# V's loads in small pieces, V's rounding on GpSimd, and first loads and scores issued ahead of a meeting

## The chip, the cores and the metric

The kernel runs on one core of one Trainium2 chip. The metric is the device time of one launch in microseconds (us). The core has five engines that run side by side, each with its own instruction stream, and that meet only at semaphores: TensorE (PE, with the weight loads shown apart as PEld), VectorE (DVE), ScalarE (ACT), GpSimd (POOL) and SyncE (SP), which here only issues DMAs. "SPq" is SyncE's queue of DMA issues.

## What is computed

64 images (3 x 96 x 96) and 64 texts of 32 tokens become one sequence each of N = 36 + 32 = 68 tokens of 192 channels. An attention of 12 heads with fake quantization follows, then a mixture of 8 experts. The part that the change touches is the attention:

```python
def fq_act(x):
    mn = jnp.minimum(x.min(), 0.0); mx = jnp.maximum(x.max(), 0.0)
    scale = jnp.maximum((mx - mn) / 255.0, EPS)
    zp = qmin - jnp.round(mn / scale)
    return (clip(round(x / scale) + zp) - zp) * scale, scale
y, _ = fq_act(x @ fq_weight(w_qkv).T + b_qkv)      # one scale for all of Q, K, V
attn, s_attn = fq_act(einsum('bhnd,bhmd->bhnm', q, k) * hd ** -0.5)   # one scale for all scores
attn = int_log_softmax(attn, s_attn)
o, _ = fq_act(einsum('bhnm,bhmd->bhnd', attn, v))
o, _ = fq_act(o @ fq_weight(w_proj).T + b_proj)
```

Each `fq_act` needs the largest and the smallest value of a whole tensor before any of it can be rounded, so the kernel comes to a halt at each of them: all engines finish, one number is formed, all go on.

## The kernel before

**Stages.** The program is one block of five streams. `barrier(eng, name)` (line 120) is a meeting of all five: each engine drains, adds one to `all_engines_done` and waits until all have. The meetings divide the program into the embedding with Q, K and V; the first pass over the scores, which forms them only to take their extremes; the second pass, which forms them again and does softmax and the sum over V; and the output projection with the experts.

**Embedding.** `STEPS` = 29 steps each handle some tiles. `UNITS_AT` says at which step which of 16 units of tokens goes through `qkv`; `scale_v` (line 1306) on VectorE multiplies its V rows into one of two buffers `vst`, and `store_v` on SyncE writes them to the DRAM tensor `v_rows`. `scale_v(e)` waits until the rows of unit e - 2 have left the buffer (`v_saved`). `load_v` brings V back with tokens in partitions, so that `yv` has 68 partitions of 64 sequences times 192 channels. `V_LOADS` (line 218) lists these loads as (step, unit that must be stored, first sequence, end). `extremes_qkv` on VectorE takes the extremes.

**First pass.** It runs in 8 chunks of 8 sequences. ScalarE's `to_halves(c)` (line 916) scales Q and K into `qt` in 8 instructions, first the columns left of a tile of 64 rows ("Q's remainder", the last 4 of 68 tokens), then the rest. VectorE's `to_whole(c)` (line 1390) rounds the remainder (`left_whole`) and the rest into the arrays QK0 and QK1 (`qk_whole`). GpSimd spreads the remainder of every chunk over 16 columns per head with `headmask` (line 758, `qk_chunk`), in two instructions, for QK0 (128 partitions) and QK1 (64). SyncE's `load_seqs` copies sequences from QK0 and QK1 to the staging tiles `st0` and `st1` (three DMAs each), waiting for `qk_whole` and `qk_chunk`; TensorE's `scores` works on two sequences at a time (`scored`), and VectorE's `extremes(c)` (line 1407) reduces them in PSUM, four instructions for each pair, 32 pairs.

After chunk 8 ScalarE converts V (`v_added`, line 940, two instructions of 6144 elements) once all chunks are done, VectorE rounds it into `VQ` (line 1432), reduces the extremes and raises `a_minmax`. GpSimd's `reduce_pair` (line 731) takes the maximum over partitions, some 60 small VectorE instructions on `sc` form the scalars of the softmax, and four constants for the output projection follow (lines 1492 to 1495). Then comes the meeting.

**Second pass.** 32 pairs of sequences. SyncE runs `load_two`, four steps later `spread_v`, which copies V from `VQ` to `stv`, and in the last step `load_rest`, two large loads for the last stage (`hf`, 3264 KB, and `w_split`, 4032 KB). VectorE works in the fixed order of the `pipeline` call at line 1570.

## Time and profile before

| what | us |
| --- | --- |
| runs | 943.77, 942.96, 940.64 |
| median | 942.96 |
| profiled execution, its time | 945.13 |
| profiled execution, its span | 943.2 |
| VectorE busy, of the span | 709.8 |
| TensorE busy | 604.6 |
| ScalarE busy | 515.3 |
| GpSimd busy | 252.1 |

The span is what the trace covers; the execution's time has 1.9 us more around it. Times in the trace count from the span's start. No engine is busy all the time, and a meeting costs what the engine that comes last is late, so the profile is to be read stretch by stretch and at the seams between stages: there the idle time ahead of a group, and the engine that ended it, tell more than sums.

### The profile page before, as it was taken

To read this page: it belongs to the slowest core of one execution; us is meant where nothing else is said; L and a number is where in the kernel's file an instruction comes from. 1 tells how busy PE (TensorE), PEld (TensorE's weight loads), DVE (VectorE), ACT (ScalarE), POOL (GpSimd) and SP (SyncE) were. 2 spreads that over 40 slices of the span, in tenths; PEclk is the share of its full clock that TensorE was granted. 3 is DMA by queue.
4 is the path that set the end of the run, shared out by engine and by line. 5 is a ranking of instruction groups with operands and counts; after the bars stand their busy time and mean duration, and the time that the engine had idled before them with its cause. 6 is when DMAs were issued, how large, how long until landed. Compare 5 with 4: busy or idle time off the path is not lost.

```text
span 943.2 us, 19819 instructions
## 1 busy us (share of the span) xinstructions
PE 604.6 (64%) x6474; PEld 451.9 (48%) x6474; DVE 709.8 (75%) x1831; ACT 515.3 (55%) x951; POOL 252.1 (27%) x245
## 2 busy tenths in 40 slices
PE   3589889898406667058888888341222349999970
PEld 2589768776204334024555555331112237777760
DVE  2535668777548999789999999987776788667783
ACT  3122268766345424048888888454554226888840
POOL 2022111120011221012222222110355750036575
PEclk9999789999755555555565555555555569999985
DMA  7974024443222221022222222451011241467753
GB/s 172 258 202 120 18 54 131 109 119 120 96 66 82 68 68 51 9 47 33 43 43 43 43 43 37 106 220 59 33 55 58 77 147 51 140 188 218 226 168 113
DMA packets 151481, 92.77 MB, mean 98 GB/s; under 512 B 88828, under 2 KB 143684, under 8 KB 151084
## 3 DMA queue, kind: packets, MB, share of 16 engines
q1 hardware_dynamic: 143560, 72.28, 29.3%
q0 software_dynamic: 7856, 19.68, 7.2%
q8 instruction: 34, 0.56, 0.3%
q14 instruction: 31, 0.25, 0.1%
HBM read 45.62 MB, written 31.85 MB: 82 GB/s over the span
## 4 chain that ended last, share of the span: by engine, by line
DVE 28%; PE 24%; issue 17%; SPq 16%; ACT 9%; DMA 3%; POOL 2%; POOLq 0%; DVEq 0%; ACTq 0%
PE ps L1844 19%; SPq L659 8%; ACT R L806 5%; ACT R L809 3%; DVE M L1413 3%; DVE M L1414 3%; SPq L637 2%; POOL R L799 2%; SPq L636 2%; SPq L638 2%; DVE R L1403 2%; DVE R L1801 1%; PE ps L2018 1%; PE ps L2114 1%; PE ps L1869 1%
## 5 line engine op out<-in xcount | busy, mean ns | idle before, releaser
L1844 PE MATMUL ps<-R 128*128 128x256 f16 (+9 forms) x2064 | 310.2, 303 | 53.0 <-DVE R L1801 16.1
L1844 PEld LDWEIGHTS ps<-R 128*128 128x128 f16 (+5 forms) x2064 | 221.6, 129 | 113.3 <-issue 59.1
L806 ACT ACTIVATE R<-ps 128x768 f16<-128x768 f16 (+7 forms) x257 | 159.8, 649 | 93.5 <-PE ps L2018 18.9
L1844 PE MATMUL ps<-M 32*128 32x68 bf16 (+4 forms) x1196 | 100.6, 242 | 117.5 <-DMA M<-R 67.2
L1844 PEld LDWEIGHTS ps<-M 32*128 32x128 bf16 (+3 forms) x1196 | 64.9, 115 | 168.9 <-issue 66.5
L809 ACT ACTIVATE R<-R,sc 128x512 f16<-128x512 f32 (+7 forms) x107 | 83.6, 838 | 105.6 <-DVE R L1403 40.1
L799 POOL DMA_INDIRECT R<-y_by_tile,M x68 | 66.7, 981 | 98.0 <-DMA y_by_tile<-R 79.4
L771 POOL TENSOR_TENSOR R<-R,M 128x884 f32<-128x884 f32 x32 | 53.2, 1664 | 145.5 <-ACT M L958 145.5
L790 POOL DMA_INDIRECT x_by_expert<-R,M x68 | 67.2, 989 | 60.3 <-DVEq L1707 40.5
L806 ACT ACTIVATE R<-R 128x512 f16<-128x512 f32 (+4 forms) x121 | 64.1, 549 | 35.3 <-DVE R L1801 34.5
L2018 PE MATMUL ps<-ident_b,R 128*68 128x128 bf16 x416 | 53.8, 298 | 25.3 <-ACT R L806 23.9
L1844 PE MATMUL ps<-M,R 128*128 128x8 f16 (+3 forms) x358 | 38.7, 242 | 30.5 <-DVE R L1603 21.9
L2018 PEld LDWEIGHTS ps<-ident_b,R 128*68 128x68 bf16 x416 | 39.6, 160 | 33.0 <-ACT R L806 29.4
L2077 PE MATMUL ps<-ident_f,R 128*128 128x128 f16 x102 | 14.0, 309 | 60.4 <-DVE R L1652 60.4
L1806 DVE TENSOR_TENSOR R<-R 128x256 f16<-128x256 f32 x58 | 24.6, 425 | 36.5 <-ACT R L806 36.5
L1844 PE MATMUL ps<-R,M 68*32 68x4 bf16 (+3 forms) x1680 | 46.7, 208 | 3.7 <-DVE R L1314 2.5
L949 ACT ACTIVATE ps<-ps,sc 128x512 f32<-128x512 f32 x64 | 37.2, 603 | 18.2 <-PE ps L1844 17.2
L1511 DVE SCALAR_TENSOR_TENSOR R<-ps,sc,M 128x544 f16<-128x544 f32 x64 | 42.5, 706 | 6.2 <-PE ps L1844 5.6
L1844 PEld LDWEIGHTS ps<-M,R 128*128 128x128 f16 (+2 forms) x358 | 25.9, 119 | 41.2 <-issue 14.8
L741 POOL COPY R<-R 96x768 f32<-96x768 f32 x24 | 20.5, 863 | 91.0 <-PE ps L1906 91.0
L1413 DVE TENSOR_REDUCE M<-ps 128x8 f32<-128x544 f32 x64 | 41.3, 645 | 4.1 <-PE ps L1844 3.9
L1844 PEld LDWEIGHTS ps<-R,M 68*32 68x32 bf16 (+1 forms) x1680 | 36.2, 111 | 11.9 <-issue 5.0
(293 smaller groups left out, 1050.2 us busy)
## 6 DMA issues: line engine op xcount, KB each, us to landing
R<-x_by_expert SPq DMA_DIRECT2D x41, 192.0 KB, 2.6
y_by_tile<-R SPq DMA_DIRECT2D x41, 192.0 KB, 2.3
R<-in_x_dram SPq DMA_DIRECT2D x12, 576.0 KB, 9.0
M<-R SPq DMA_DIRECT2D x16, 260.0 KB, 2.3
M<-R SPq DMA_DIRECT2D x32, 130.0 KB, 2.0
R<-w_split SPq DMA_DIRECT2D x1, 4032.0 KB, 23.1
R<-h_rows SPq DMA_DIRECT2D x1, 3264.0 KB, 14.3
out_dram<-R SPq DMA_DIRECT2D x17, 192.0 KB
```

The costliest lines, as they stand in the source:

```text
L659: sp.dma_start(stv[:, par, b, a].rearrange("p (j h d) -> p j h d", h=2, d=HD)[:, :, a, :], VQ[:, bass.ds(g * 2 + b, 1), :].rearrange("p o ...
L771: pool.tensor_tensor(L[par], L[par], S[:, par, 1, :].unsqueeze(2).to_broadcast([P, SLOTS, N]), ALU.subtract).then_inc(sem("relative"), 1)
L790: pool.indirect_dma_start(xg, bass.IndirectOffsetOnAxis(ap=slot[:, n, k:k + 1], axis=0), rows2[:, n, :], None).then_inc(sem("scattered"), 16)
L799: pool.indirect_dma_start(gb[:, i % 4, j, k, :], None, yg[0:TILE * ready, :], bass.IndirectOffsetOnAxis(ap=y_slot[:, 2 * i + j, k:k + 1], ...
L806: return act.activation(out_, in_, ACT.Copy)
L809: return act.activation(out_, in_, ACT.Identity, scale=scale, bias=bias)
L949: act.activation(rem[:, cols], rem[:, cols], ACT.Square, bias=s1(A_BH)).then_inc(sem("sq"), 1)
L1413: dve.tensor_reduce(rowmax[:, g:g + 1, s0:s0 + 2 * k].rearrange("p o (a s) -> p (o a) s", a=2), sv, X, ALU.max)
L1414: last = dve.tensor_reduce(gmin[:, g * 2 + part:g * 2 + part + 1], sv, mybir.AxisListType.XYZ, ALU.min)
L1511: last = dve.scalar_tensor_tensor(D[:, s0:s0 + 2 * k, :].rearrange("p (a s) k -> p a s k", a=2), score_part(0, part), s1(A_NKK), m.unsquee ...
L1844: return pe.matmul(o, a, b, start=start, stop=stop, skip_group_check=True)
L2018: last = pe.transpose(pPT[:, i, :], slots(Pb[par])[:, at, :], ident_b[:, :])
```

## The change

It has these parts.

1. The 64 sequences of V are loaded in 15 pieces instead of 5. Five of them, for sequences 6 to 32, stay on SyncE at steps 20 and 24. The other ten (`V_LATE`, of 2 or 4 sequences) are issued by ScalarE between its chunks 1 to 6 of the first pass. SyncE ends the embedding with waits for all stores, without a load.
2. VectorE spreads Q's remainder for chunk 0; GpSimd begins with chunk 1.
3. The rounding of V into `VQ` is an instruction of GpSimd after its last spread and ahead of `reduce_pair`; SyncE's first `spread_v` waits for it (`v_whole`).
4. The output constants are computed by VectorE after its second chunk, before the first extremes.
5. `barrier` can take work to be issued between reporting and waiting. SyncE issues the loads of the second pass's first two pairs there, TensorE the scores of the first pair; at the next meeting SyncE issues the loads of `load_rest` there.

GpSimd between the first and the second pass, before the change. `sc<-sc` is the reduce over partitions, and a row with ISA alone is an instruction that sets up GpSimd's routines:

```order
L733 ISA
L733 ISA sc<-sc 128x2 [waits a_minmax]
L774 MEMSET M 68x1536 [waits all_engines_done]
L771 ISA
L771 TENSOR_TENSOR R<-R,M 128x884 [waits log_w,log_sum] x2
```

and after it:

```order
L763 TENSOR_TENSOR R<-R,headmask 128x8x64 [waits left_whole]
L763 TENSOR_TENSOR R<-R,headmask 64x8x64 [waits scored]
L770 TENSOR_SCALAR R<-R,sc 68x12288 [waits v_added]
L738 ISA
L738 ISA sc<-sc 128x2 [waits a_minmax]
L781 MEMSET M 68x1536 [waits all_engines_done]
L778 ISA
L778 TENSOR_TENSOR R<-R,M 128x884 [waits log_w,log_sum] x2
```

The rounding of V stands between the last spread and the setup for the reduce.

SyncE in the last steps of the embedding, before (`R<-v_rows` is a load of V, `v_rows<-R` a store, `M<-R` a score load):

```order
L607 DMA R<-v_rows 68x3072 [waits v_saved0,v_saved1,w_stored1,w_stored0]
L607 DMA R<-v_rows 68x1152 [waits v_saved1,v_saved0,h_out]
L600 DMA v_rows<-R 16x6x192 [waits v_scaled]
L600 DMA v_rows<-R 16x6x192 x2
L596 DMA v_rows<-R 4x32x192 [waits v_scaled]
L596 DMA v_rows<-R 4x32x192
L600 DMA v_rows<-R 16x6x192 [waits v_scaled]
L600 DMA v_rows<-R 16x6x192 x2
L607 DMA R<-v_rows 68x3072 [waits qkv_extremes,v_saved0,h_stored1,v_saved1,h_stored0,t_stored]
L636 DMA M<-R 128x1040 [waits qk_chunk,qk_whole,all_engines_done]
```

and after:

```order
L599 DMA v_rows<-R 4x32x192 [waits v_scaled]
L599 DMA v_rows<-R 4x32x192
L603 DMA v_rows<-R 16x6x192 [waits v_scaled]
L603 DMA v_rows<-R 16x6x192 x2
L599 DMA v_rows<-R 4x32x192 [waits v_scaled]
L599 DMA v_rows<-R 4x32x192
L603 DMA v_rows<-R 16x6x192 [waits v_scaled]
L603 DMA v_rows<-R 16x6x192 x2
L634 DMA M<-R 128x1040 [waits h_stored1,w_stored0,v_saved1,v_saved0,w_stored1,h_stored0,t_stored,qk_chunk,qk_whole,all_engines_done]
```

Three V loads are gone from among the stores, and the waits for the stores now come before the meeting.

VectorE at the start of the first pass, before (4 remainder columns, then 128 and 68 of the rest):

```order
L1396 TENSOR_SCALAR R<-R,sc 128x8x4 [waits vector_step,left_added,all_engines_done]
L1396 TENSOR_SCALAR R<-R,sc 64x8x4
L1403 TENSOR_SCALAR R<-R,sc 128x8x128 [waits q_added]
L1403 TENSOR_SCALAR R<-R,sc 128x8x68
L1403 TENSOR_SCALAR R<-R,sc 64x8x128 [waits q_added]
L1403 TENSOR_SCALAR R<-R,sc 64x8x68
L1396 TENSOR_SCALAR R<-R,sc 128x8x4 [waits left_added]
L1396 TENSOR_SCALAR R<-R,sc 64x8x4
```

and after:

```order
L1406 TENSOR_SCALAR R<-R,sc 128x8x4 [waits vector_step,left_added,all_engines_done]
L1406 TENSOR_SCALAR R<-R,sc 64x8x4
L1411 TENSOR_TENSOR R<-R,headmask 128x8x64 [waits left_whole]
L1411 TENSOR_TENSOR R<-R,headmask 64x8x64
L1420 TENSOR_SCALAR R<-R,sc 128x8x128 [waits q_added]
L1420 TENSOR_SCALAR R<-R,sc 128x8x68
L1420 TENSOR_SCALAR R<-R,sc 64x8x128 [waits q_added]
L1420 TENSOR_SCALAR R<-R,sc 64x8x68
L1406 TENSOR_SCALAR R<-R,sc 128x8x4 [waits left_added]
L1406 TENSOR_SCALAR R<-R,sc 64x8x4
```

Two multiplications by `headmask` stand between the remainder and the rest of chunk 0.

The diff:

```diff
--- before.py
+++ after.py
@@ -117,11 +117,13 @@
 
         barriers = {}
 
-        def barrier(eng, name):
+        def barrier(eng, name, ahead=None):
 
             n = barriers.get(name, 0) + 1
             barriers[name] = n
             eng.drain().then_inc(sem("all_engines_done"), 1)
+            if ahead:
+                ahead()
             eng.wait_ge(sem("all_engines_done"), 5 * n)
 
         h_dram = nc.dram_tensor("h_rows", [T, C], F32, kind="Internal").ap()
@@ -215,7 +217,8 @@
         XSTEP = [k // 2 for k in range(16)] + [6 * q + 8 + w // 3 for q in range(3) for w in range(6)] + [23, 23, 23, 25, 25, 25]
         UNITS_AT = {2: 0, 3: 1, 4: 2, 5: 3, 6: 4, 7: 5, 10: 8, 11: 9, 16: 10, 17: 11, 22: 12, 23: 13, 24: 6, 25: 14, 26: 7, 27: 15}
         UNIT_ORDER = [UNITS_AT[k] for k in sorted(UNITS_AT)]
-        V_LOADS = [(20, 11, 24, 32), (24, 12, 6, 24), (26, 6, 32, 48), (26, 6, 0, 6), (None, 15, 48, B)]
+        V_LOADS = [(20, 11, 24, 28), (20, 11, 28, 32), (24, 12, 6, 12), (24, 12, 12, 18), (24, 12, 18, 24)]
+        V_LATE = [(1, 0, 4), (1, 4, 6), (2, 32, 36), (2, 36, 40), (3, 40, 44), (3, 44, 48), (4, 48, 52), (4, 52, 56), (5, 56, 60), (6, 60, B)]
         LN_TILES = [(0, 16), (16, 22), (22, 28), (28, 34), (34, 37), (37, 40)]
         LN_STEP = [-1, 6, 12, 18, 21, 24]
         WSTEP = [9, 12, 13, 18, 19, 21]
@@ -612,12 +615,7 @@
                     load_images(2 + s // 6)
                 for at, unit, first, end in V_LOADS:
                     if s == at:
-                        if end == 48:
-                            for a in range(2):
-                                sp.wait_ge(sem(f"w_stored{a}"), 16 * sum(WCH_DMAS[a::2]))
-                        if first == 0:
-                            sp.wait_ge(sem("h_out"), 16 + 4 * GRID)
-                        load_v(first, end, UNIT_ORDER.index(unit) if unit < 15 else 15)
+                        load_v(first, end, UNIT_ORDER.index(unit))
                 if s - 2 in WSTEP:
                     store_split(WSTEP.index(s - 2))
                 if s in (7, 13, 19, 25):
@@ -627,8 +625,8 @@
             sp.wait_ge(sem("t_stored"), 16 * 16)
             for a in range(2):
                 sp.wait_ge(sem(f"h_stored{a}"), 32)
-            sp.wait_ge(sem("qkv_extremes"), 16)
-            load_v(48, B, 15)
+                sp.wait_ge(sem(f"v_saved{a}"), v_stores(16 + a))
+                sp.wait_ge(sem(f"w_stored{a}"), 16 * sum(WCH_DMAS[a::2]))
             barrier(sp, "sp")
 
 
@@ -647,30 +645,37 @@
                 load_seqs(par, bass.ds(g * 4, 4), 4)
 
             def load_two(g, par, half):
+                if isinstance(g, int) and g < 2:
+                    return
                 wait(sp, "scored", 32 + g - 1)
                 load_seqs(par, bass.ds(g * 2, 2), 2)
 
+            def load_ahead():
+                for g in range(2):
+                    wait(sp, "scored", 32 + g - 1)
+                    load_seqs(g, slice(g * 2, g * 2 + 2), 2)
+
             pipeline(sp, [(load_four, 0)], 16)
-            barrier(sp, "sp")
+            barrier(sp, "sp", load_ahead)
             def spread_v(g, par, half):
+                if isinstance(g, int) and g == 0:
+                    sp.wait_ge(sem("v_whole"), 1)
                 wait(sp, "o_summed", g - 1)
                 for b in range(2):
                     for a in range(2):
                         sp.dma_start(stv[:, par, b, a].rearrange("p (j h d) -> p j h d", h=2, d=HD)[:, :, a, :],
                                      VQ[:, bass.ds(g * 2 + b, 1), :].rearrange("p o (j h d) -> p (o j) h d", h=2, d=HD)[:, :, a, :]).then_inc(sem(f"v_spread{par}"), 16)
 
-            def load_rest(g, par, half):
-
-                if not (isinstance(g, int) and g == 31):
-                    return
+            def load_rest():
+
                 for k in range(2):
                     sp.wait_ge(sem(f"st_qk{k}"), 24 * 48)
                 sp.dma_start(hf, h_dram.rearrange("(i p) c -> p i c", p=P)).then_inc(sem("hf"), 16)
                 sp.dma_start(wsplit, w_dram).then_inc(sem("w_split"), 16)
 
             sp.wait_ge(sem("v_cleared"), 1)
-            pipeline(sp, [(load_two, 0), (spread_v, 4), (load_rest, 4)], 32)
-            barrier(sp, "sp")
+            pipeline(sp, [(load_two, 0), (spread_v, 4)], 32)
+            barrier(sp, "sp", load_rest)
 
             sp.wait_ge(sem("zeros"), 1)
             for k in range(E - 1):
@@ -750,7 +755,7 @@
             barrier(pool, "pool")
 
 
-            for c in range(8):
+            for c in range(1, 8):
                 pool.wait_ge(sem("left_whole"), c + 1)
                 for k, (_, _, QK, rows, _) in enumerate(QKPARTS):
                     if k == 1:
@@ -761,6 +766,8 @@
                                               ALU.mult)
                 last.then_inc(sem("qk_chunk"), 1)
 
+            pool.wait_ge(sem("v_added"), 2)
+            pool.tensor_scalar(VQ, vt, sc[0:N, Q_CAPM:Q_CAPM + 1], H16 + 512.0, ALU.min, ALU.subtract).then_inc(sem("v_whole"), 1)
             reduce_pair(A_MX, "a_minmax")
             barrier(pool, "pool")
 
@@ -931,10 +938,13 @@
 
             for c in range(8):
                 to_halves(c)
+                for at, first, end in V_LATE:
+                    if c == at:
+                        act.dma_start(yv[:, first:end, :], v_dram[:, first:end, :]).then_inc(sem("v_in"), 16)
 
             act.wait_ge(sem("qk_whole"), 8)
             act.wait_ge(sem("qk_chunk"), 8)
-            act.wait_ge(sem("v_in"), 16 * len(V_LOADS))
+            act.wait_ge(sem("v_in"), 16 * len(V_LOADS + V_LATE))
             for n in range(2):
                 bs = slice(32 * n, 32 * n + 32)
                 ident_(vt[:, bs, :], yv[:, bs, :], scale=s1(Q_INV, N), bias=s1(T2, N)).then_inc(sem("v_added"), 1)
@@ -1395,6 +1405,13 @@
                     left = qt[rows, par, k, :, 2 * NQ:2 * NQ + NL]
                     last = ts(left, left, sc[rows, Q_CAPM:Q_CAPM + 1], H16 + 512.0, ALU.min, ALU.subtract)
                 last.then_inc(sem("left_whole"), 1)
+                if c == 0:
+                    dve.wait_ge(sem("left_whole"), 1)
+                    for k, (_, _, QK, rows, _) in enumerate(QKPARTS):
+                        last = tt(QK[rows, b8, 2 * NQ:3 * NQ].rearrange("p b (h i) -> p b h i", i=NL),
+                                  qt[rows, 0, k, :, 2 * NQ:2 * NQ + NL].unsqueeze(2).to_broadcast([rows.stop, 8, 16, NL]),
+                                  headmask[rows, k, :].unsqueeze(1).unsqueeze(3).to_broadcast([rows.stop, 8, 16, NL]), ALU.mult)
+                    last.then_inc(sem("qk_chunk"), 1)
                 for k, (_, _, QK, rows, krows) in enumerate(QKPARTS):
                     dve.wait_ge(sem("q_added"), 2 * c + k + 1)
                     t = qt[:, par, k]
@@ -1403,6 +1420,12 @@
                         last = ts(dst, src, sc[r, Q_CAPM:Q_CAPM + 1], H16 + 512.0, ALU.min, ALU.subtract)
                 last.then_inc(sem("qk_whole"), 1)
 
+
+            def output_constants():
+                for k, (lo, hi) in enumerate(((C1, C1 + 3), (C1 + 1, P), (C1 + 2, P))):
+                    ch(dve.tensor_reduce(bmask[:, k:k + 1], ident[:, lo:hi], X, ALU.add, negate=k > 0))
+                ch(dve.reciprocal(vrow, prow))
+                ch(tt(bprow, bprow, vrow, ALU.mult))
 
             def extremes(c):
                 for i in range(4):
@@ -1426,10 +1449,10 @@
             for c in range(9):
                 if c < 8:
                     to_whole(c)
+                if c == 1:
+                    output_constants()
                 if c >= 1:
                     extremes(c - 1)
-            dve.wait_ge(sem("v_added"), 2)
-            ts(VQ, vt, s1(Q_CAPM, N), H16 + 512.0, ALU.min, ALU.subtract)
             dve.wait_ge(sem("extremes"), 32)
             ch(dve.tensor_reduce(s1(A_MX), rowmax, XY, ALU.max))
             ch(ts(s1(A_MX), s1(A_MX), 0.0, None, ALU.max))
@@ -1489,10 +1512,6 @@
             ch(dve.tensor_copy(ident_h, ident[:, :]))
             ch(ts(minus_a, ident[:, :], s1(A_NA), None, ALU.mult))
             ch(dve.memset(s1(A_PB), 128.0 * (127.0 + 1.0 + H16) + 64.0))
-            for k, (lo, hi) in enumerate(((C1, C1 + 3), (C1 + 1, P), (C1 + 2, P))):
-                ch(dve.tensor_reduce(bmask[:, k:k + 1], ident[:, lo:hi], X, ALU.add, negate=k > 0))
-            ch(dve.reciprocal(vrow, prow))
-            ch(tt(bprow, bprow, vrow, ALU.mult))
             barrier(dve, "dve")
 
             dve.wait_ge(sem("rmq"), 1)
@@ -1994,13 +2013,20 @@
                     wait(pe, "extremes", g * 2 + k - 1)
                     scores(g * 2 + k, 4 * k, par, 2 * k, 2)
 
+            def scores_ahead():
+                pe.wait_ge(sem("st_qk0"), 9 * 48)
+                pe.wait_ge(sem("extremes"), 31)
+                scores(0, 0, 0, 0, 1)
+
             def second_scores(g, par, half):
+                if isinstance(g, int) and g == 0:
+                    return
                 pe.wait_ge(sem(f"st_qk{par}"), (8 + half + 1) * 48)
                 wait(pe, "dist", g)
                 scores(g, 0, par, 0, 1)
 
             pipeline(pe, [(first_scores, 0)], 16)
-            barrier(pe, "pe")
+            barrier(pe, "pe", scores_ahead)
 
             def remainders(g, par, half):
                 pe.wait_ge(sem("quot"), g + 1)
```

## Rows read from the trace of the kernel before

**Rows 1.** Busy time by stretches: the columns are named in the first line.

```profile
core 0: us, PE busy (x) PEld busy (x) DVE busy (x) ACT busy (x) POOL busy (x), PEclk, DMA share, GB/s
...
251.30:263.80 12.50, 0.00 (x0) 0.00 (x0) 0.01 (x1) 0.00 (x0) 0.00 (x0) 0.62 0.24 82
...
287.00:378.80 91.80, 60.47 (x621) 38.76 (x620) 91.29 (x164) 36.41 (x42) 16.38 (x13) 0.50 0.22 61
```

**Rows 2.** VectorE in time: start, us, engine, line, operation, tiles, idle before and releaser.

```profile
250.76 0.54 DVE L1327 TENSOR_REDUCE R<-R 128x1 f32<-128x384 f32 x1
263.80 0.55 DVE L1314 CUSTOM_DVE_ANT_1 R<-ps,M 96x384 f32<-96x384 f32 x1 [12.49 <-DMA v_rows<-R]
```

**Rows 3.** SyncE's queue at the end of the embedding, in time.

```profile
245.66 0.63 SPq L607 DMA_DIRECT2D R<-v_rows  x2
246.34 1.85 SPq L600 DMA_DIRECT2D v_rows<-R  x3
248.94 8.52 SPq L596 DMA_DIRECT2D v_rows<-R  x2
264.66 1.84 SPq L600 DMA_DIRECT2D v_rows<-R  x3
268.00 0.25 SPq L607 DMA_DIRECT2D R<-v_rows  x1
```

**Rows 4.** VectorE at the start of the first pass, in time.

```profile
273.56 0.76 DVE L1403 TENSOR_SCALAR R<-R,sc 128x1024 bf16<-128x1024 f16 x2 [1.70 <-ACT R L809]
275.81 0.86 DVE L1403 TENSOR_SCALAR R<-R,sc 64x1024 bf16<-64x1024 f16 x2 [1.50 <-ACT R L809]
...
280.95 2.18 DVE L1403 TENSOR_SCALAR R<-R,sc 64x1024 bf16<-64x1024 f16 x2 [1.50 <-ACT R L809]
287.04 0.72 DVE L1413 TENSOR_REDUCE M<-ps 128x8 f32<-128x544 f32 x1 [3.90 <-PE ps L1844]
```

**Rows 5.** GpSimd in time, from the first meeting to the second.

```profile
268.15 0.37 POOL L733 PARTITION_ALL_REDUCE sc<-sc  x1 [60.05 <-DVEq L1380]
279.40 3.07 POOL L758 TENSOR_TENSOR R<-R,headmask 128x512 bf16<-128x512 f16 x3 [10.88 <-issue]
...
296.58 1.50 POOL L758 TENSOR_TENSOR R<-R,headmask 128x512 bf16<-128x512 f16 x1 [6.56 <-DVE R L1396]
...
383.64 0.38 POOL L733 PARTITION_ALL_REDUCE sc<-sc  x1 [23.01 <-DVEq L1438]
```

**Rows 6.** GpSimd in time, its first reduce over partitions.

```profile
96.33 0.38 POOL L729 PARTITION_ALL_REDUCE sc<-sc  x1 [7.55 <-DVEq L1214]
```

**Rows 7.** GpSimd's groups by form: busy us, mean ns of one, idle before.

```profile
L771 POOL TENSOR_TENSOR R<-R,M 128x884 f32<-128x884 f32 x32 | 53.2, 1664 | 145.5 <-ACT M L958 145.5
L741 POOL COPY R<-R 96x768 f32<-96x768 f32 x24 | 20.5, 863 | 91.0 <-PE ps L1906 91.0
...
L774 POOL MEMSET M<- 68x1536 bf16 x1 | 1.4, 1375 | 12.3 <-DVEq L124 12.3
```

**Rows 8.** ScalarE in time, its conversion of V.

```profile
360.83 10.91 ACT L809 ACTIVATE R<-R,sc 68x6144 f16<-68x6144 f32 x2 [19.65 <-DVE R L1403]
```

**Rows 9.** VectorE in time, its rounding of V.

```profile
378.88 3.42 DVE L1432 TENSOR_SCALAR R<-R,sc 68x12288 bf16<-68x12288 f16 x1
```

**Rows 10.** VectorE in time, the output constants.

```profile
393.77 0.66 DVE L1493 TENSOR_REDUCE M<-ident 128x1 f32<-128x3 f32 x3
...
395.85 0.36 DVE L1495 TENSOR_TENSOR M<-M 128x192 f32<-128x192 f32 x1
```

**Rows 11.** VectorE in time, the first distances of the second pass.

```profile
402.88 1.33 DVE L1511 SCALAR_TENSOR_TENSOR R<-ps,sc,M 128x544 f16<-128x544 f32 x2 [4.55 <-PE ps L1844]
```

**Rows 12.** SyncE, VectorE and GpSimd in time, at the end of the second pass.

```profile
604.93 8.73 SPq L669 DMA_DIRECT2D R<-w_split  x1
...
612.18 0.17 DVE L1577 TENSOR_SCALAR sc<-sc 128x2 f32<-128x2 f32 x1
...
613.97 0.38 POOL L733 PARTITION_ALL_REDUCE sc<-sc  x1 [17.50 <-SPq L124]
```

## The prediction, as written before the run

> **What bounds the kernel now.** I read the table by stretches first [rows 1], because one average over six stages says nothing about a change that touches two meetings of the engines. It shows a stretch of 12.5 us (251.3 to 263.8) in which no engine computes, and, from 287.0 to 378.8, the first pass over the scores with VectorE busy for 91.29 of 91.80 us. So in the first pass only VectorE's own work and its start count. Then I read the idle gap before each VectorE group at the seams, since a gap names its releaser.
>
> At the first seam VectorE finishes at 251.3 and starts again at 263.80 after 12.49 us idle, released by a store into v_rows [rows 2]. It is `scale_v` of the last unit, which waits until the V rows two units earlier have left their buffer. The SyncE queue shows why they are late: the two V loads of step 26 (16 and 6 sequences) are issued at 245.66, the three stores at 246.34 come behind them, and the next two stores take 8.52 us to issue [rows 3]. The loads move 82 GB/s with a quarter of the DMA engines' time [rows 1], so 22 sequences, 1122 KB, take 1122/82 = about 13.7 us; the stores sit behind that.
>
> At the second seam (start of the first pass) the first extremes start at 287.04, after 3.90 us of waiting for TensorE [rows 4]. The first score load waits for GpSimd, whose first spread starts only at 279.40, with 10.88 us of idle time that the profile calls issue [rows 5]. At the third seam (after the last extremes) VectorE does V's pass, 3.42 us [rows 9], then its small reductions; GpSimd's reduce over partitions runs at 383.64 [rows 5]; scalars and constants follow until 396.2 [rows 10]; and the first distances start at 402.88, after 4.55 us idle [rows 11]. At the fourth, VectorE is ready at 612.35, but the reduce starts at 613.97, released by SyncE, which spent 8.73 us issuing the load of the split weights [rows 12].
>
> **The change part by part.** Times below are on the old clock, so a step that starts 12.4 us earlier only because the first wait is gone keeps its old time.
>
> 1. V loads leave SyncE's queue ahead of the last stores: the 12.49 us go. What is late next? TensorE and VectorE both finish their previous work at about 251.3 [rows 1, 2], so nothing fills the gap. SyncE's last stores were issued at 264.66 and over 1.84 us, and it could issue its next load, which waits for them, at 268.00 [rows 3], before GpSimd's reduce at 268.15 [rows 5] and the scalars behind it that VectorE brings to the meeting; moved with VectorE it stays behind cover. Term: -12.4 us.
>
> 2. VectorE spreads the first eight sequences. Two instructions of 512 elements; a VectorE TENSOR_TENSOR of 192 elements took 0.36 us [rows 10], 1.9 ns an element, so each costs at most 0.96 us and both 1.9 us, and there are 1.70 us of idle time just there, waiting for ScalarE [rows 4]. I take nothing; without that cover it is up to 1.9 us. The first load is now released by VectorE's own last piece at 276.7 instead of by GpSimd's second instruction at about 281.5, so the scores would be there at 287.04 - 4.8 = 282.2. VectorE is later: the pieces of the second chunk start at 280.95 and took 2.18 us beside GpSimd's spreads; the same two took 0.86 us for the first chunk without them [rows 4]. GpSimd then has a single spread in that place, so I take 281.8. Behind them now stand the output constants, from 393.77 to 396.21, 2.44 us [rows 10]. Extremes start at 284.3 instead of 287.04: -2.7 us, kept to the end of the pass because VectorE is full.
>
> 3. ScalarE issues ten small V loads between its conversions. ScalarE is far ahead of VectorE in the pass (36.41 us of work in 91.8 us [rows 1]), so issue time is hidden. The loads share DMA engines with the score loads: 38 sequences are 1938 KB, 23.6 us at 82 GB/s [rows 1]. If every microsecond of it came between scores it would cost 23.6 us; I take zero, since pieces of at most 204 KB (2.5 us each) leave room between themselves, and keep 3 us for the range.
>
> 4. V's pass moves from VectorE (3.42 us) to GpSimd, ahead of the reduce in the same queue, with the reduce's configuration instruction between the two. ScalarE's V conversion ended at 360.83 + 10.91 = 371.7 [rows 8], now 2.7 us earlier, 369.0. GpSimd's pass over 12288 elements is not in the trace. Bounds from its rows [rows 7]: 0.90 ns an element (MEMSET, 1375 ns for 1536) gives 11.0 us; COPY, 863 ns for 768, gives 1.12 ns and 13.8 us; two inputs, 1664 ns for 884, give 1.88 ns and 23.1 us; a spread beside VectorE, 1.50 us for 512, gives 2.93 ns and 36 us [rows 5]. It has one input, so I take 12 us, between the first two: it ends at 381.0.
>
> The Trainium skill bears on this pass. In "GPSIMD Engine Reference", section 3.1, a body of at most two operations runs at 1.03 cycles an element and a tight loop otherwise at 1.8 cycles at best; at 1.2 GHz that is an estimated 10.5 or 18.4 us here. By the first the sum would be 1.5 us lower, by the second 6.4 us higher.
>
> 5. After the pass comes the change of GpSimd's routine. What the trace shows: after the first reduce, the spread started 10.9 us after the reduce ended and 7.5 us after VectorE's left columns had released it (273.56 - 1.70 = 271.86 [rows 4]); for the first reduce of all, 7.55 us passed between the instruction before and its start [rows 6], and there the wait for VectorE may have hidden everything. So the switch costs between 0 and 10.9 us here, and nothing hides it now, since it stands behind the pass; before, 23 us of idle time did. I take 7.5 us. The reduce starts at 381.0 + 7.5 + 0.1 = 388.6, although VectorE has its extremes ready at about 377.4 (378.8 - 2.7, and 1.3 us of small reductions, as between the end of V's pass at 382.3 and 383.6 [rows 5, 9]). Against 383.64 that is +5.0 us, with the 2.7 us of part 2 and the 3.42 us of V's pass already in it.
>
> The Trainium skill, "GPSIMD Engine Reference", section 2.1, says that the first call to a freshly loaded routine pays about 6 us without an instruction in the profile. The gap of 10.88 us called issue fits that kind of stall. By its figure the sum would be an estimated 1.5 us lower.
>
> 6. The output constants are gone from behind the reduce: -2.4 us (their cost is in part 2).
>
> 7. The first loads and scores of the second pass are made ahead of the meeting. They need only finished chunks and free banks, all there before GpSimd's reduce. VectorE has nothing more to do ahead of them from 402.88 - 4.55 = 398.33 on; those 4.55 us go [rows 11]. Next late would be VectorE itself. Term: -4.5 us. If the second pass took it back through a queue that stays late, 0.
>
> 8. The two large loads are issued after SyncE has reported to the last meeting: the reduce follows VectorE at 612.45 instead of 613.97 [rows 12], -1.5 us. They are issued no later than before.
>
> Sum: -12.4 + 5.0 - 2.4 - 4.5 - 1.5 = -15.8 us. The profiled execution took 945.13 us (span 943.2), so 929.3 us on its terms; it stands 2.2 us above the median of 942.96, from which the same sum gives 927.2. I take 928.
>
> **The rivals.**
> *GpSimd is quick.* Pass 11.0 us, switch free or short: the reduce starts near 380.1, 8.5 us earlier than in my sum, about 919.5. For it: the first reduce of all showed no delay behind its release [rows 6]. Against: the 10.88 us [rows 5]. 0.17.
>
> *GpSimd is slow.* The pass runs at the two-input rate, 23.1 us: +11.1, about 939. At 18.5 us, midway from 13.8 to 23.1, it would be 934.5. For it: two operations and a conversion per element, which no one-input row has. 0.25 for everything from 933 to 940.
>
> *The wait is only renamed.* The stores of SyncE stay behind the loads of step 24, now three, and VectorE waits as long as before: 12.4 us less gain, 940.4. Against: those are the same bytes as before, and SyncE may issue at 245.66 [rows 3] only once the V stores ahead have landed, so the queue had drained by then. With other small mishaps, no measurable change: 0.05.
>
> *Slower.* GpSimd's pass at the rate that its spreads show beside VectorE's, 2.93 ns an element [rows 5], 36 us: the sum becomes +8.2, about 952. It decides from 27.8 us on, or 2.26 ns an element, all behind 369.0 where VectorE has nothing else to do. Against: VectorE then reads its inputs from PSUM and goes idle. 0.05.
>
> **How the numbers follow.** My forecast (924 to 933) has 0.48. The range leaves out the slower case and the unchanged one, and takes in quick and slow GpSimd and the 3 us of part 3: 918.5 to 939.5. Faster by over 0.3% (about what a measurement of this kernel tells from no change; below 940.1): 0.48 + 0.17 + 0.25 = 0.90; within: 0.05; slower: 0.05.
>
> **What would show it.** The idle before the last `scale_v` below 1 us; the first extremes 2.7 us nearer to the meeting; one GpSimd TENSOR_SCALAR of about 12 us, then idle of about 7.5 us called issue before the reduce; the wait of VectorE for that reduce about 11 us; distances right behind VectorE's small instructions; the fourth reduce 0.1 us after VectorE. I am wrong if the pass is far from 12 us, if the switch is free, or if VectorE shows gaps for TensorE in the first pass where it had none.

## The result and the profile after

The changed kernel takes 965.89 us (median of 4 runs, 965.04 to 968.13), against 943.37 us for the kernel before in the runs beside it (940.64 to 947.03). The ratio is 1.024, with a 95% interval of 1.020 to 1.028: slower, where I had forecast faster. The profiled executions have spans of 943.2 and 963.2 us, so 20.0 us are to be found in the two traces.

The first seam, VectorE at the last `scale_v` (start, duration, engine, line, operation; idle before it would stand in brackets). This row answers to [rows 2]:

```profile
246.43 0.54 DVE L1324 CUSTOM_DVE_ANT_1 R<-ps,M 96x384 f32<-96x384 f32 x1
```

The wait of 12.49 us is gone, as forecast. The first reduce runs at 250.78 instead of 268.15; 12.4 us of that are the wait, and 4.97 us stem from the embedding, which ran through earlier in this execution. I count that as no effect of the change: in the traces of the ten kernels with this same embedding, this one included, the reduce runs anywhere from 250.8 to 256.3, and this one is the earliest.

The start of the first pass on GpSimd and VectorE, in the place of [rows 4, 5]:

```profile
250.78 0.37 POOL L738 PARTITION_ALL_REDUCE sc<-sc  x1 [45.86 <-DVEq L1390]
254.51 1.28 DVE L1411 TENSOR_TENSOR R<-R,headmask 128x512 bf16<-128x512 f16 x2
256.18 0.76 DVE L1420 TENSOR_SCALAR R<-R,sc 128x1024 bf16<-128x1024 f16 x2 [0.39 <-ACT R L816]
270.25 0.73 DVE L1436 TENSOR_REDUCE M<-ps 128x8 f32<-128x544 f32 x1 [3.35 <-PE ps L1863]
```

VectorE's spreads take 1.28 us and lie in the 1.70 us in which it waited before: of these, 0.39 are left. But from the reduce to the first extremes there are now 19.47 us, against 18.89 before, where I had forecast 16.2.

VectorE's waits from the start of the first pass to the scalars behind it (waiter, line, who is waited for: us in total, times, longest):

```profile
DVE sc L1464 <- POOL sc L738: 39.8, 1, 39.8
DVE M L1436 <- PE ps L1863: 13.6, 6, 4.2
```

Two waits matter. VectorE waits 39.8 us for GpSimd's reduce, and 13.6 us for scores in the pass, where it had waited 3.9 before [rows 4]. The third seam, after the last extremes, on GpSimd, to be read beside [rows 5, 8, 9]:

```profile
352.02 10.91 ACT L816 ACTIVATE R<-R,sc 68x6144 f16<-68x6144 f32 x2 [16.69 <-DVE R L1420]
363.03 41.65 POOL L770 TENSOR_SCALAR R<-R,sc 68x12288 bf16<-68x12288 f16 x1 [11.21 <-ACT R L816]
410.74 0.37 POOL L738 PARTITION_ALL_REDUCE sc<-sc  x1 [6.06 <-issue]
411.15 0.16 DVE L1464 TENSOR_TENSOR sc<-sc 128x1 f32<-128x1 f32 x1 [39.83 <-POOL sc L738]
422.98 1.33 DVE L1530 SCALAR_TENSOR_TENSOR R<-ps,sc,M 128x544 f16<-128x544 f32 x2
```

The pass over V takes 41.65 us, 3.39 ns an element, and with the routine switch behind it VectorE stands still from 371.3 on. The distances follow with no gap (the 4.55 us of [rows 11] are gone).

In the first pass TensorE's gaps stand beside DMA issues. TensorE, then ScalarE's queue of V loads (ACTq L943), then SyncE's queue of score loads (SPq L634), then what ScalarE's arithmetic and SyncE wait for:

```profile
283.82 3.84 PE L1863 MATMUL ps<-M 32*128 32x68 bf16 x40 [6.87 <-DMA M<-R]
299.68 3.84 PE L1863 MATMUL ps<-M 32*128 32x68 bf16 x40 [7.28 <-DMA M<-R]
...
273.21 0.63 ACTq L943 DMA_DIRECT2D R<-v_rows  x2
288.85 0.62 ACTq L943 DMA_DIRECT2D R<-v_rows  x2
...
273.37 0.54 SPq L634 DMA_DIRECT2D M<-R  x1
289.01 0.52 SPq L634 DMA_DIRECT2D M<-R  x1
...
288.83 0.41 ACT L816 ACTIVATE R<-R,sc 128x32 f16<-128x32 f32 x1 [10.53 <-POOL R L763]
...
SPq L642 <- POOL R L763: 48.1, 7, 9.8
```

V loads belong to six chunks. In the last four of them they are issued 0.15 or 0.16 us ahead of a score load, and TensorE then waits for it: 6.87 and 7.28 us where two V loads go, 3.89 and 4.47 us (at 312.15 and 325.20) where one does. GpSimd's spread releases both: the copy of the scores' operands, and ScalarE's next chunk, whose V loads its queue issues at once, although they stand behind the chunk's arithmetic in the code (issue at 288.85, 0.02 us after that arithmetic starts; it lasts some 5 us). The first two chunks are different: there the V loads are issued 0.92 us ahead of a score load (258.45 and 259.37) and 0.68 us behind one (263.60 and 262.92). The first scores start at 268.18, 8.8 us after their load was issued; in the kernel before it was 3.5 us (281.55 and 285.05). A window of 15 us there (us, busy time of each engine, TensorE's granted clock, the DMA engines' mean busy share, GB/s):

```profile
273.00:288.00 15.00, 7.68 (x80) 5.01 (x80) 11.07 (x22) 5.10 (x8) 1.90 (x3) 0.50 0.31 82
```

VectorE is busy for 11.07 of 15 us and the DMA engines are not: a share of 0.31.

### The profile page after: what moved, and what is told of

The parts are those of the page before. It is cut to its first block, busy times and chain, and to the rows that moved or that the text cites. A ratio compares the mean times of both kernels' runs of the same rounds, so it can differ in the third digit from the quotient of the medians.

```text
span 963.2 us, 19831 instructions
## 1 busy us (share of the span) xinstructions
PE 596.6 (62%) x6474; PEld 447.2 (46%) x6474; DVE 704.1 (73%) x1832; ACT 515.2 (53%) x951; POOL 291.0 (30%) x244
## 4 chain that ended last, share of the span: by engine, by line
DVE 32%; PE 23%; issue 16%; ACT 11%; POOL 7%; DMA 7%; SPq 2%; DVEq 1%; ACTq 1%; POOLq 0%
PE ps L1863 18%; ACT R L813 5%; POOL R L770 4%; DMA M<-R 4%; ACT R L816 4%; POOL R L806 2%; DVE R L1530 2%; DMA R<-in_L_txt_tok_embed_dram,R 2%; DVE M L1560 2%; DVE M L1579 2%; DVE R L1555 2%; DVE R L1820 2%; PE ps L2044 1%; DVE R L1543 1%; DVE R L1537 1%
## 5 line engine op out<-in xcount | busy, mean ns | idle before, releaser
L1863 PE MATMUL ps<-R 128*128 128x256 f16 (+9 forms) x2064 | 303.9, 299 | 107.4 <-DVE R L1543 63.3
L1863 PEld LDWEIGHTS ps<-R 128*128 128x128 f16 (+5 forms) x2064 | 217.7, 127 | 166.3 <-issue 116.1
L813 ACT ACTIVATE R<-R 128x512 f16<-128x512 f32 (+4 forms) x121 | 64.1, 549 | 34.5 <-DVE R L1820 33.4
L1436 DVE TENSOR_REDUCE M<-ps 128x8 f32<-128x544 f32 x64 | 41.2, 644 | 13.7 <-PE ps L1863 13.6
L770 POOL TENSOR_SCALAR R<-R,sc 68x12288 bf16<-68x12288 f16 x1 | 41.6, 41648 | 11.2 <-ACT R L816 11.2
L1863 PEld LDWEIGHTS ps<-M,R 128*128 128x128 f16 (+2 forms) x358 | 25.2, 118 | 40.4 <-issue 13.3
```

The costliest lines, as they stand in the source:

```text
L770: pool.tensor_scalar(VQ, vt, sc[0:N, Q_CAPM:Q_CAPM + 1], H16 + 512.0, ALU.min, ALU.subtract).then_inc(sem("v_whole"), 1)
L813: return act.activation(out_, in_, ACT.Copy)
L1436: dve.tensor_reduce(rowmax[:, g:g + 1, s0:s0 + 2 * k].rearrange("p o (a s) -> p (o a) s", a=2), sv, X, ALU.max)
L1863: return pe.matmul(o, a, b, start=start, stop=stop, skip_group_check=True)
```

## The experiments

All are ratios to the kernel before on the same chip. Differences in us between two kernels are differences of their medians; the intervals of the ratios are 2 to 5 us to each side, so such a difference is good to a few us, and where it matters the traces are read beside it. Four experiments came first, to part the two suspects.

**V's rounding back on VectorE.** The rest of the change stays.

```diff
-            pool.wait_ge(sem("v_added"), 2)
-            pool.tensor_scalar(VQ, vt, sc[0:N, Q_CAPM:Q_CAPM + 1], H16 + 512.0, ALU.min, ALU.subtract).then_inc(sem("v_whole"), 1)
+            dve.wait_ge(sem("v_added"), 2)
+            ts(VQ, vt, s1(Q_CAPM, N), H16 + 512.0, ALU.min, ALU.subtract).then_inc(sem("v_whole"), 1)
```

> The changed kernel, with V's rounding given back to VectorE, behind its last extremes as before the change. Theory A (the pass on GpSimd and the routine switch behind it are the loss): the third reduce follows VectorE's end of the extremes by 3.4 + 1.4 us instead of 40.7 us, so about 36 us less than the changed kernel, 930 us. Rival (another wait, hidden under the pass, comes up, such as the switch alone with its 6 us): 936 us or more, with idle time called issue ahead of the reduce. If the late V loads cost nothing, 919 us.

Measured: 929.08 us (927.65 to 931.62), ratio 0.983 [0.978, 0.988]. The one instruction is worth 36.8 us, together with the routine switch that it brought into the open; from the reduce at the start of the first pass to the one at its end, the two traces differ by 37.7 us. VectorE does it in 3.42 us and waits 0.6 us for the reduce; its waits for scores in the pass remain:

```profile
370.89 3.42 DVE L1455 TENSOR_SCALAR R<-R,sc 68x12288 bf16<-68x12288 f16 x1
...
DVE M L1434 <- PE ps L1863: 11.9, 5, 3.7
DVE sc L1464 <- POOL sc L738: 0.6, 1, 0.6
```

**The ten late V loads cut into 64 and 4 partitions.** GpSimd keeps the rounding.

```diff
-                        act.dma_start(yv[:, first:end, :], v_dram[:, first:end, :]).then_inc(sem("v_in"), 16)
+                        for r in (slice(0, 64), slice(64, N)):
+                            act.dma_start(yv[r, first:end, :], v_dram[r, first:end, :]).then_inc(sem("v_in"), 16)
```

> The changed kernel, with each of the ten late V loads cut by partitions into two loads of 64 and 4 rows, same bytes. Theory B (a load of 68 rows runs on four of the DMA engines, since the share is 0.25 while one runs, and the score loads that start with it wait on those four): 64 rows spread over all engines, the pieces are through in under 1 us, the gaps of VectorE in the first pass (13.6 us) go back to the 4 us of before or less: about 11 us less than the changed kernel, 955 us. Rival (the bytes or ScalarE's issuing cost the time): unchanged, 966 us, or a little slower from ten more issues.

Measured: 955.69 us (952.39 to 957.38), ratio 1.011 [1.008, 1.014]; 10.2 us less than the change, and 12.8 us less from reduce to reduce in the traces. The same bytes in more DMAs, and no wait for scores is left in the list of VectorE's waits; the pass over V is as long as before. The same window, now with VectorE nearly full; its DMA share of 0.52 is higher in part because the pass gets along faster and 1.5 times the bytes move in it (123 GB/s against 82):

```profile
273.00:288.00 15.00, 9.79 (x101) 6.26 (x100) 14.85 (x29) 7.53 (x12) 2.54 (x2) 0.50 0.52 123
...
DVE sc L1465 <- POOL sc L738: 39.8, 1, 39.8
```

So the loads of 68 partitions held up the score loads; that they did so by running on few of the DMA engines is the reading that fits. The windows can't show which engines those were. The Trainium skill, "DMA: Bandwidth & Descriptors", in its section on why a DMA increments its semaphore by 16, says that a DMA is spread over the largest number of engines up to 16 that divides the outer dimensions of both its sides; that makes 4 for 68 partitions and 16 for 64. A busy share of 0.24 in [rows 1] and this experiment agree with it. So does a count of packets: on ScalarE's queue the ten uncut loads make 720 packets, 680 with data and 40 of 4 bytes, four a load; cut, 880, 680 with data and 200 of 4 bytes, 20 a pair. That these small packets count the engines is a reading, but 4 and 16 + 4 are the page's numbers.

**Both.**

> The changed kernel with both edits: V's rounding on VectorE and the late V loads cut into 64 and 4 rows. If both theories hold and add up: 966 - 36 - 11 = 919 us, 2.5% less than the kernel before. If the two losses overlap: 925 to 930 us.

Measured: 919.48 us (917.04 to 920.94), ratio 0.972 [0.967, 0.977]. The two effects add: 36.8 + 10.2 = 47.0 from the single edits, 46.4 found (from reduce to reduce 37.7 + 12.8 = 50.5 and 48.1). No version of the study is faster by more than the noise.

**The kernel before with its V loads cut into 64 and 4 partitions**, and nothing else.

```diff
-                sp.dma_start(yv[:, first:end, :], v_dram[:, first:end, :]).then_inc(sem("v_in"), 16)
+                for r in (slice(0, 64), slice(64, N)):
+                    sp.dma_start(yv[r, first:end, :], v_dram[r, first:end, :]).then_inc(sem("v_in"), 16)
```

> The kernel before, with nothing but each of its five V loads cut into 64 and 4 rows. Theory B: the stores behind the two loads of step 26 are no longer held up, the 12.5 us of idle time ahead of the last scale_v go, 931 us. Rival (the queue is held up by the number of bytes, or by the loads' place ahead of the stores): 943 us, the gap stays.

Measured: 931.96 us (930.94 to 932.80), ratio 0.986 [0.981, 0.991]. The cut alone brings 12.4 us, without moving a load:

```profile
DVE R L1315 <- DMA v_rows<-R: 2.4, 1, 2.4
...
247.57 1.15 SPq L596 DMA_DIRECT2D v_rows<-R  x2
```

Of the 12.49 us wait [rows 2] 2.4 are left, and the two stores that took 8.52 us to issue [rows 3] take 1.15. The last stores had been late because the V loads were slow, and these were slow for their 68 partitions. The plainest row is the load of the last 16 sequences, which runs with no other DMA beside it. First the kernel before, then this one, each with the window in which the load moves its bytes (the columns of [rows 1]) and its packets (counted over a longer window):

```profile
268.60:279.80 11.20, 0.00 (x0) 0.00 (x0) 4.69 (x21) 9.09 (x15) 0.40 (x1) 0.50 0.24 75
DMA packets 72, 0.84 MB, mean 64 GB/s; under 512 B 4, under 2 KB 4, under 8 KB 4
...
257.50:261.60 4.10, 0.00 (x0) 0.00 (x0) 1.62 (x11) 2.45 (x5) 0.00 (x0) 0.50 0.91 204
DMA packets 88, 0.84 MB, mean 72 GB/s; under 512 B 20, under 2 KB 20, under 8 KB 20
```

The same 0.84 MB take some 11 us at 75 GB/s with a share of 0.24, and cut some 4 us at 204 GB/s with 0.91. Of the small packets there are 4 and 20 again.

The second group asks why the pass is slow and why the score loads are late, and takes two smaller terms apart.

**Why score loads are late: ScalarE issues them at another time.** On the version with the rounding on VectorE (loads uncut), ScalarE issues a chunk's V loads only when its own arithmetic for that chunk is finished, some 5 us after the release:

```diff
+                if any(c == at for at, _, _ in V_LATE):
+                    act.wait_ge(sem("q_added"), 2 * c + 2)
```

> e_round_dve (V's rounding on VectorE, ten late loads of 68 rows on ScalarE), with one more wait: ScalarE issues a chunk's V loads only when its own conversions of that chunk are done, some 5 us after the event that releases them and the score load together. Theory B2 (it is the coincidence with the score load that costs): VectorE's gaps in the first pass go from 12 us to 0 to 4 us, 919 to 923 us. Rival (V's bytes cost as much at any moment): 929 us.

Measured: 921.52 us (920.43 to 923.13), ratio 0.976 [0.973, 0.979]; 7.6 us less than without the wait (that run was on another chip, with the kernel before at 944.32 there and 944.27 here). VectorE's waits for scores fall from 11.9 to 2.5 us:

```profile
DVE M L1436 <- PE ps L1865: 2.5, 1, 2.5
...
287.26 0.63 ACTq L943 DMA_DIRECT2D R<-v_rows  x2
287.36 0.52 SPq L634 DMA_DIRECT2D M<-R  x1
```

The one wait that is left follows the one place where the wait in the code did not keep the two apart: V loads issued 0.10 us ahead of a score load, after which TensorE stands until 297.39 for a score load and VectorE until 299.38. The same loads on as few engines cost about 2 us, 921.52 against 919.48 with cut loads, when they mostly don't start together with a score load. It takes both to lose the time: a load that occupies few engines for long, and its issue by the event that also issues what TensorE needs next.

**Spread of chunk 0 back on GpSimd**, on the fastest version.

```diff
-            for c in range(1, 8):
+            for c in range(8):
...
-                if c == 0:
-                    dve.wait_ge(sem("left_whole"), 1)
-                    for k, (_, _, QK, rows, _) in enumerate(QKPARTS):
```

> e_both with the spread of the first eight sequences given back to GpSimd. By the row of b_rows64 GpSimd can start 7 us after the meeting; the first score load goes about 3 us later, VectorE's pieces of chunk 1 run beside the spreads again (2.2 instead of 0.85 us), and the first extremes start 1.3 to 2 us later: 921 us. If VectorE's spread were what keeps the first pass early, 4.8 us: 924 us. If GpSimd's switch of routine is no longer than the wait for VectorE, no difference: 919.5 us.

Measured in one run: 919.36 us, span 917.5 against 917.8. From the reduce to the first extremes it takes 16.55 us instead of 16.16, so VectorE's spreads bring 0.4 us:

```profile
256.34 0.37 POOL L738 PARTITION_ALL_REDUCE sc<-sc  x1 [47.85 <-DVEq L1389]
265.18 3.07 POOL L763 TENSOR_TENSOR R<-R,headmask 128x512 bf16<-128x512 f16 x3 [8.46 <-issue]
272.89 0.72 DVE L1428 TENSOR_REDUCE M<-ps 128x8 f32<-128x544 f32 x1 [0.41 <-PE ps L1857]
```

GpSimd starts its spreads 8.84 us after the reduce started, where the kernel before needed 11.25 [rows 5] and the same kernel with cut V loads 9.48. The stall that I wanted to go around had shrunk with the V loads; that they delayed GpSimd's routine is a reading, since no record names what GpSimd waits for there.

**No loads and scores ahead of the meeting**, on the fastest version.

```diff
-            barrier(sp, "sp", load_ahead)
+            barrier(sp, "sp")
...
-            barrier(pe, "pe", scores_ahead)
+            barrier(pe, "pe")
```

> e_both without the work ahead of the second meeting: the first two score loads and the first scores of the second pass come after it again (the late issue of the two large loads stays). VectorE idles about 4.5 us ahead of the first distances: 924 us. If the second pass is limited by SyncE's queue and not by its start, the 4.5 us come back in it: 919.5 us.

Measured: 920.68 us (919.28 to 922.34), ratio 0.974 [0.971, 0.977], against 0.972 [0.967, 0.977]: the times alone don't tell the two apart. The trace does. From the end of the last extremes to the first distances it takes 21.3 us instead of 17.0, with this wait in it:

```profile
DVE R L1529 <- PE ps L1862: 4.3, 1, 4.3
```

The profiled span is 2.7 us longer, with an embedding 1.5 us shorter. So the wait costs its 4.3 us and they are still there at the end (4.3 - 1.5 = 2.8). The medians differ by only 1.2 us, with ranges that overlap, since the embedding varies by more than this term.

**What makes GpSimd's pass slow.** Eleven further GpSimd instructions at the seam of the fastest version, each waited for, their results unused:

> The version of e_both with eleven extra GpSimd instructions into dead memory, after V's rounding on VectorE and ahead of the third reduce, each waited for, 768 elements a row where not said otherwise: the rounding as in the change (768 and 1536 elements, 68 rows), the same on 128 rows of bf16, with two constants, with the minimum alone, from f32 to f32, f32 minimum alone, multiply and add with constants, copy f16 to bf16, copy f32, product of two f16 inputs. The time of the run says nothing, the durations do. Theory C (two operations with a conversion cost it, per element): 2.6 us for 768 elements and 5.2 us for 1536 at 3.39 ns, the single operation and the copies 0.8 us (1.1 ns an element). Rival (the scalar that is read from memory costs it): the forms with constants fall to about 1 ns. Rival (the size of the one instruction does): 768 elements cost under 1.5 us. Idle time called issue of about 6 us stands ahead of the reduce in each case.

Time of this kernel (951.59 us) says nothing; the durations do. In order: the rounding over 768, over 1536, from bf16 with 128 partitions, with two constants; min alone; the rounding in f32; min by a constant in f32; multiplication and addition of two constants; two copies; a product of two tensors:

```profile
365.79 2.87 POOL L782 TENSOR_SCALAR R<-R,sc 68x768 bf16<-68x768 f16 x1 [21.78 <-DVE R L1480]
368.75 5.44 POOL L783 TENSOR_SCALAR R<-R,sc 68x1536 bf16<-68x1536 f16 x1
374.28 2.88 POOL L784 TENSOR_SCALAR R<-R,sc 128x768 bf16<-128x768 bf16 x1
377.24 2.77 POOL L785 TENSOR_SCALAR R<-R 68x768 bf16<-68x768 f16 x1
380.11 2.20 POOL L786 TENSOR_SCALAR R<-R,sc 68x768 bf16<-68x768 f16 x1
382.40 2.85 POOL L787 TENSOR_SCALAR R<-R,sc 68x768 f32<-68x768 f32 x1
385.34 2.12 POOL L788 TENSOR_SCALAR R<-R 68x768 f32<-68x768 f32 x1
387.55 0.83 POOL L789 TENSOR_SCALAR R<-R 68x768 bf16<-68x768 f16 x1
388.45 0.82 POOL L790 CAST R<-R 68x768 bf16<-68x768 f16 x1
389.33 0.82 POOL L791 COPY R<-R 68x768 f32<-68x768 f32 x1
390.24 1.63 POOL L792 TENSOR_TENSOR R<-R 68x768 bf16<-68x768 f16 x1
```

The rounding is slow at any size, from 3.7 ns an element with the start in it at 768 to 3.39 at 12288; for min and subtraction, type, partitions and per-partition scalar don't matter (2.77 to 2.88 us). VectorE and TensorE are idle here but for 0.9 us of VectorE in 26, and the DMA share is 0.00, so contention is out. One TENSOR_SCALAR is as quick as a copy: the one with a multiplication and an addition. My theory that two operations and a conversion make the price fell with it, for that one has them too.

**Which operations are quick.** Ten more, in the same way: subtraction of a constant, addition of one; multiplication by, subtraction of and max with a per-partition scalar; multiplication by such a scalar and subtraction of a constant; multiplication by 1 and addition of the negative constant; min and multiplication; the quick form over 1536; a difference of two tensors.

> The fastest version so far with ten more GpSimd instructions over 68x768 (one 68x1536) elements at the seam between the two passes, each waited for, nothing of them used; what counts is the duration of each. Theory (GpSimd has a quick path for addition, subtraction and multiplication, and min and max leave it): a subtraction or addition of a constant 0.8 us, a multiplication by a per-partition scalar 0.8, subtraction of one 0.8, max 2.2, multiplication and subtraction 0.8, multiplication by 1 and addition of the negative constant 0.8, min and multiplication 2.9, the 1536 elements 1.6, the difference of two tensors 1.6. Rival (a per-partition scalar or a subtraction is what costs): those with a pointer or with a subtraction take 2.2 to 2.9 us, those with a constant and an addition 0.8.

Measured (the kernel took 948.22 us, which again says nothing):

```profile
364.49 2.17 POOL L782 TENSOR_SCALAR R<-R 68x768 bf16<-68x768 f16 x1 [21.77 <-DVE R L1479]
366.75 2.14 POOL L783 TENSOR_SCALAR R<-R 68x768 bf16<-68x768 f16 x1
...
373.60 2.21 POOL L786 TENSOR_SCALAR R<-R,sc 68x768 bf16<-68x768 f16 x1
375.90 2.86 POOL L787 TENSOR_SCALAR R<-R,sc 68x768 bf16<-68x768 f16 x1
378.84 0.83 POOL L788 TENSOR_SCALAR R<-R 68x768 bf16<-68x768 f16 x1
379.76 2.86 POOL L789 TENSOR_SCALAR R<-R,sc 68x768 bf16<-68x768 f16 x1
```

Both theories of this run fail. It is not min that is slow, since a lone addition of a constant takes 2.14 us as well; nor the pointer, since min and subtraction are slow with two constants too (2.77 us). Every single operation took 2.1 to 2.2 us and every pair 2.8 to 2.9, save the one pair of a multiplication and an addition with both numbers constant. Neither two constants with another pair that has no min (multiplication and subtraction, say) nor a multiplication and an addition with a per-partition scalar were tried, so why that one pair is quick stays open.

**The pass in the quick form.** The changed kernel with its late V loads cut, without the cap (which bears only on values that round past the largest step):

```diff
-            pool.tensor_scalar(VQ, vt, sc[0:N, Q_CAPM:Q_CAPM + 1], H16 + 512.0, ALU.min, ALU.subtract).then_inc(sem("v_whole"), 1)
+            pool.tensor_scalar(VQ, vt, 1.0, -(H16 + 512.0), ALU.mult, ALU.add).then_inc(sem("v_whole"), 1)
```

> The changed kernel with its late V loads cut into 64 and 4 rows, and with GpSimd's pass over V written as a multiplication by 1 and an addition of a constant instead of the smaller of the value and the cap, less a constant. The cap is left out, which bears only on values that round past the largest step. Theory (the operation min is what is slow on GpSimd: min alone took 2.20 us for 768 elements and min with a subtraction 2.87, a multiplication and an addition 0.83 on the same operands): the pass over 12288 elements takes 0.83 x 16 = 13.3 us instead of 41.65, starts at 352 and ends at 365.3, the reduce still starts 6.0 us behind it, at 371.3 instead of 399.66, and VectorE waits some 11.5 us for it instead of 39.8. Time 955.7 - 28.3 = 927. Rival (the whole pass is slow for its size or because it works beside VectorE and TensorE, whatever its operation): 41 us again, time 955 to 956. Second rival (the pass is short, and the 6 us behind it belong to the slow pass): reduce at 365.5, time 921.

Measured: 924.39 us (922.46 to 924.74), ratio 0.979 [0.977, 0.981]; 31.3 us less than with min and subtraction.

```profile
351.38 10.43 POOL L770 TENSOR_SCALAR R<-R 68x12288 bf16<-68x12288 f16 x1 [11.20 <-ACT R L816]
368.17 0.37 POOL L738 PARTITION_ALL_REDUCE sc<-sc  x1 [6.37 <-issue]
```

The pass takes 10.43 us, 0.85 ns an element, in its place in the kernel, with VectorE at work beside some 8 us of it (its last reduction ends at 359.5). That is less than the 13.3 us expected, which were scaled up from 768 elements with the start in them; over 1536 the form took 1.47 us. The rival, a pass that is slow for its size or its neighbours, falls. The switch stays, 6.37 us, so it does not belong to the slow pass. And even so the rounding is better placed on VectorE: 919.5 against 924.4.

## Why the prediction was wrong

At the third seam (the prediction's count) the reduce was forecast for 388.6 on the old clock, 376.2 with the first wait gone, and ran at 410.74. The difference of 34.5 us has four parts: embedding -4.97, V's conversion on ScalarE 11.3 late (it ended at 362.93, forecast 356.6 - 4.97), the pass +29.65, the switch -1.44.

1. *The stores' wait, -12.4*: right; idle before `scale_v` is 0. What I gave as its cause, that loads stand ahead of stores, was half of it: the loads were slow for their shape, and cutting them brings 12.4 us in the place where they are, 10.1 of it in this wait. (The working has a slip without weight: 1122 KB are 1149 thousand bytes, 14.0 us at 82 GB/s.)
2. *First extremes 2.7 us nearer to the reduce*: wrong in the changed kernel (0.6 us farther). The first score load was issued 4.8 us nearer to the reduce, as forecast, but it was slow beside the V loads. With them cut, the extremes are 18.89 - 16.16 = 2.7 us nearer. That the number fits is luck: the spreads on VectorE bring 0.4 of it, and without them GpSimd's spread starts 8.84 us after the reduce instead of 11.25, a gain that the prediction did not have. In the changed kernel the constants are hidden by VectorE's wait for the scores.
3. *Late V loads, put at zero, 3 us for the range*: this step failed. They cost 13.6 us of waits for scores, and V's conversion came 11.3 us late. I divided bytes by 82 GB/s and reasoned from the room between pieces. [rows 1] had the warning in it: 82 GB/s with a share of 0.24 is a load that holds a quarter of the engines, not one that leaves the others' work alone. Pieces of 2.5 us don't collide by chance either: one event released both issues.
4. *The pass, 12 us*: this step failed most, 41.65. I chose the row nearest in the count of inputs (MEMSET and COPY), when no row showed TENSOR_SCALAR on GpSimd. My widest bound, 36 us, came from a spread beside VectorE and was exceeded too. The rival "slower" had the right place and sense; I gave it 0.05, against it that VectorE would be idle. It was idle, from 371.3 on, and that did not help. Its threshold of 27.8 us left out the V loads: with their loss beside it the change loses from a pass of an estimated 41.65 - 22.5 = 19 us on (22.5 us is what it lost, and 31.2 us off the pass took 31.3 off the time). The Trainium skill, "GPSIMD Engine Reference", section 3.1, gives 1.03 cycles an element for at most two operations; by it the pass would be an estimated 10.5 us. The form with a multiplication and an addition of constants took 10.43 us and agrees; the form in this kernel, two operations as well, took four times that and does not.
5. *The switch, 7.5*: 6.06, and 5.8 to 6.4 in the four other kernels with GpSimd work right ahead of the reduce. The sense was right, and it is paid in full as nothing hides it. "GPSIMD Engine Reference", section 2.1, of the Trainium skill has about 6 us for the first call of a freshly loaded routine, and these rows agree.
6. *Constants, -2.4*: right. 7. *Ahead of the meeting, -4.5*: right; no gap before the distances, 4.3 us in the run without. 8. *Large loads after the report, -1.5*: right; VectorE ends at 632.91 and the reduce follows 0.28 us later, 1.62 before [rows 12]:

```profile
632.74 0.17 DVE L1596 TENSOR_SCALAR sc<-sc 128x2 f32<-128x2 f32 x1
633.19 0.37 POOL L738 PARTITION_ALL_REDUCE sc<-sc  x1 [16.16 <-DVEq L124]
```

Two of the three signs of being wrong that the prediction names came true: the pass is far from 12 us, and VectorE has gaps for TensorE in the first pass. The sum of -15.8 with 34.5 added gives +18.7, and the spans differ by 20.0; the rest of 1.3 us, behind the distances, is within what such executions vary. With the two failed steps mended the change gives 919.5, 24.8 us less than the kernel before, of which 12.4 are to be had by cutting five loads.

## What to carry over

Before work is moved to an engine on which the trace has no row of that very instruction with those operations, measure it alone; neighbours that read the same amount can be four times as quick. A transfer's share of the DMA engines belongs beside its rate: here 75 GB/s at a share of 0.24, with no other transfer running, went with a shape that kept it on few engines, and cutting it brought as much as the wait that a rearrangement of the queues was meant to remove. Where one event releases two queues, look whether their transfers start together each time, however much room there is on average.

## What the hardware showed

- GpSimd, 768 elements per partition, TENSOR_SCALAR in the forms tried: one operation 2.12 to 2.21 us, two 2.77 to 2.88, a multiplication and an addition of constants 0.83, like a copy (0.82); a product of two tensors 1.63.
- VectorE does the same rounding over 12288 elements in 3.42 us, GpSimd in 41.65.
- Between GpSimd's elementwise work and its reduce over partitions, where nothing hides it, lie 5.8 to 6.4 us.
- A V load of 16 sequences into 68 partitions, alone: 75 GB/s at a DMA share of 0.24; the same bytes as 64 and 4 partitions: 204 GB/s at 0.91.
- With V loads of 68 partitions issued 0.15 or 0.16 us ahead of a score load, TensorE was idle for 6.87 and 7.28 us (two V loads), 3.89 and 4.47 us (one). Cutting the loads took 12.4 us off the kernel before and 10.2 off the changed one.
